# Two attention stages on one core: the end of the first attention reordered, and at the end of the second a bank for the last maxima and two sums through TensorE and ScalarE

## What is computed

```python
tgt2 = heads16_attention(x, ctx, Wq, Wk, Wv)[0]
y = x + tgt2
norm_X = layernorm(ctx, norm1)
norm_F_L = layernorm(y, norm2)
attended = attention(norm_F_L, norm_X, norm_X, 256 ** -0.5)      # first attention
h = gelu(attended @ fc1_w.T + fc1_b)                              # width 4
cross_attended = h @ fc2_w.T + fc2_b
norm_cross = layernorm(cross_attended, norm3)
self_attended = attention(norm_cross, norm_cross, norm_cross, 256 ** -0.5)   # second attention
out = norm_F_L + gamma2 * (cross_attended + gamma1 * self_attended)
```

## Time and profile before

| | us |
|---|---|
| median of 3 runs | 238.35 |
| lowest and highest | 234.89, 239.81 |
| profiled execution, its own time | 236.88 |
| its span, first to last instruction | 234.8 |
| PE, DVE, ACT, POOL busy in it | 209.6, 182.5, 153.8, 146.7 |

### The profile page before, as it was taken

The page is one execution under the profiler, slowest core; times in us unless marked ns, Lnnn a source line. Parts: engine busy times, 40 slices in busy tenths (PEclk is TensorE's granted clock), DMA queues, the critical chain, the costliest instruction groups (busy, mean ns, idle before and its releaser), DMA issues.

```text
span 234.8 us, 4965 instructions
## 1 busy us (share of the span) xinstructions
PE 209.6 (89%) x1730; PEld 151.6 (65%) x1730; DVE 182.5 (78%) x360; ACT 153.8 (66%) x295; POOL 146.7 (62%) x240
## 2 busy tenths in 40 slices
PE   8999979987779999999999989997998898899760
PEld 8776646776556978789787867794766444454230
DVE  6499977779979988878778999993333867988673
ACT  2177865544546877778777896789558786677520
POOL 6536551467499999987987793934953288322320
PEclk9999999999999999999999999999999999999855
DMA  6990000084540554426535200000000004444458
GB/s 227 384 332 4 1 1 3 0 223 138 178 179 3 179 179 138 149 78 180 179 108 158 94 3 0 6 0 1 3 0 0 3 15 167 179 181 180 183 212 324
DMA packets 14712, 26.81 MB, mean 114 GB/s; under 512 B 1760, under 2 KB 1760, under 8 KB 14688
## 3 DMA queue, kind: packets, MB, share of 16 engines
q1 hardware_dynamic: 14400, 25.98, 32.3%
q10 hardware_dynamic: 288, 0.52, 0.7%
HBM read 18.11 MB, written 8.39 MB: 113 GB/s over the span
## 4 chain that ended last, share of the span: by engine, by line
PE 53%; DVE 20%; ACT 10%; POOL 8%; issue 6%; DVEq 0%; ACTq 0%; POOLq 0%
PE psum L1085 15%; PE psum L1022 9%; PE psum L1093 5%; DVE xN L381 4%; DVE bn L361 4%; PE psum L970 3%; PE psum L1123 3%; DVE Fall L596 2%; DVE hmax L399 2%; PE psum L1105 2%; PE psum L1205 2%; DVE nmax L523 2%; ACT L862 2%; PE psum L1238 1%; ACT E L887 1%
## 5 line engine op out<-in xcount | busy, mean ns | idle before, releaser
L1085 PE MATMUL psum<-XT,Fall 128*128 128x256 f32 x256 | 61.0, 381 | 1.7 <-ACT Fall L857 1.7
L1085 PEld LDWEIGHTS psum<-XT,Fall 128*128 128x128 f32 x256 | 46.1, 190 | 7.3 <-ACT Fall L857 2.3
L700 POOL TENSOR_SCALAR cN<-cN,nmean,rstd 128x256 f32<-128x256 f32 x64 | 37.4, 594 | 2.5 <-POOL rstd L687 2.1
L680 POOL TENSOR_TENSOR xN<-xN,tgt 128x512 f32<-128x512 f32 x28 | 35.6, 1277 | 4.8 <-DVE xN L381 4.8
L687 POOL TENSOR_TENSOR rstd<-vps,minus_half 128x8 f32<-128x8 f32 (+1 forms) x16 | 24.2, 1512 | 19.9 <-DVE vps L372 19.6
L887 ACT ACTIVATE E<-psum,nmax 128x256 f32<-128x256 f32 x64 | 26.8, 474 | 11.9 <-DVE nmax L523 11.9
L880 ACT ACTIVATE PT<-psum 128x512 f32<-128x512 f32 x32 | 19.1, 598 | 22.7 <-PE psum L1093 22.6
L523 DVE TENSOR_REDUCE nmax<-psum 128x2 f32<-128x512 f32 x32 | 22.0, 687 | 14.7 <-PE psum L1085 14.2
L381 DVE TENSOR_SCALAR xN<-xN,bn,rstd 128x256 f32<-128x256 f32 x64 | 32.8, 558 | 0.5 <-POOL rstd L687 0.4
L581 DVE TENSOR_REDUCE nm<-psum 128x4 bf16<-128x1024 f32 x16 | 19.5, 1220 | 8.2 <-PE psum L1173 8.2
L854 ACT ACTIVATE XT<-psum,b1s,w1s 128x512 f32<-128x512 f32 x32 | 23.0, 795 | 4.0 <-PE psum L1022 4.0
(11 more groups left out here) (173 smaller groups left out, 351.9 us busy)
## 6 DMA issues: line engine op xcount, KB each, us to landing
cN<-ctx SPq DMA_DIRECT2D x32, 256.0 KB, 3.0
xN<-x SPq DMA_DIRECT2D x32, 256.0 KB, 4.1
out<-Fall SPq DMA_DIRECT2D x32, 256.0 KB, 2.3
x0T<-x0t ACTq DMA_DIRECT2D x1, 256.0 KB, 3.0
c0T<-c0t ACTq DMA_DIRECT2D x1, 256.0 KB, 3.9
wqT<-wqt SPq DMA_DIRECT2D x1, 256.0 KB, 3.6
wkT<-wkt SPq DMA_DIRECT2D x1, 256.0 KB, 4.1
wvT<-wvt SPq DMA_DIRECT2D x1, 256.0 KB, 4.8
```

Source lines behind the costliest of these rows:

```text
L680: pool.tensor_tensor(xN[:, b % SLOTS, :], xN[:, b % SLOTS, :], tgt2[:, :, :].rearrange("p t d -> p (t d)"), ALU.add).then_inc(y_ok, 1)
L700: pool.tensor_scalar(own, own, nmean[:, p % 4, NT * m + t:NT * m + t + 1], root_of(p, 0, m, t), ALU.add, ALU.mult)\
L1085: last = pe.matmul(bank[SBANK1[b % 3]][:, t * N:(t + 1) * N], Fall[:, b, c, t * P:(t + 1) * P], XT[:, p % 4, c, m * N:(m + 1) * N], start= ...
```

## The change

The program of PE, ACT and DVE is reordered at the end of the first attention and at the start of the second, and the end of the second attention gets three things: `maxima_turn(15)` writes in bank 3, once `weights(14)` has read that bank, and no longer in bank 5; the sums of pairs 13 and 15 leave DVE, in that PE first loads `Fall` into their result banks by matmuls with the identity (`load`), `output` adds onto that, and ACT copies the sum back over `Fall` (`moved`); and SP waits for `moved_ok` for these two pairs, in the same order of stores as before.

```diff
+    LOADED = (13, 15)
+    def maxima_bank(p):
+        return bank[3 if p == PAIRS - 1 else 5][0:2 * VW, 0:P // 2].bitcast(BF16)
...
         for n, b in ((n, b) for n in STORED for b in (2 * n, 2 * n + 1)):
-            sp.wait_ge(fin_ok, n + 1 + (b == B - 1))
+            if n in LOADED:
+                sp.wait_ge(moved_ok, 2 * LOADED.index(n) + b % 2 + 1)
+            else:
+                sp.wait_ge(fin_ok, min(n, 13) + 1)
...
         def finish(n):
             dve.wait_ge(f_mm, n + 1)
-            if n < PAIRS - 1:
-                dve.tensor_tensor(pair(n), results(n), pair(n), ALU.add).then_inc(fin_ok, 1)
-            else:
-                for m in range(2):
-                    own = Fall[:, 2 * n + m, :, :].rearrange("p c n -> p (c n)")
-                    dve.tensor_tensor(own, bank[result(n)[m]], own, ALU.add).then_inc(fin_ok, 1)
+            dve.tensor_tensor(pair(n), results(n), pair(n), ALU.add).then_inc(fin_ok, 1)
         maxima(0)
-        saved(QUADS - 1)
...
-            if p >= 5:
+            if p >= 5 and p - 5 not in LOADED:
                 finish(p - 5)
             if p == 0:
+                saved(QUADS - 1)
                 hidden_input(2)
...
-            if b >= 1:
+            if 1 <= b < B - 2:
                 weights_copied(b - 1)
+            if b == B - 3:
+                turned_values(QUADS - 1)
             exponentials(b)
-            if b % 4 == 1 and q >= 1:
+            if b % 4 == 1 and 1 <= q < QUADS - 1:
                 turned_values(q)
             if b % 4 == 2 and q >= 1:
                 applied(q - 1)
+            if b >= B - 2:
+                weights_copied(b - 1)
...
+        def moved(n):
+            act.wait_ge(f_mm, n + 1)
+            for m in range(2):
+                act.activation(Fall[:, 2 * n + m, :, :].rearrange("p c n -> p (c n)"), bank[result(n)[m]], ACT.Copy)\
+                    .then_inc(moved_ok, 1)
         for p in range(2 * QUADS + 4):
-            if p < PAIRS:
+            if p < PAIRS - 1:
                 maxima_turned(p)
             if p == 0:
+                weights(0)
                 applied(QUADS - 1)
+            if p + 2 < PAIRS:
+                turned(p + 2)
+            if 1 <= p < PAIRS:
+                weights(p)
             if p == 1:
                 hidden(2)
-            if p + 2 < PAIRS:
-                turned(p + 2)
-            if p < PAIRS:
-                weights(p)
+            if p == PAIRS - 2:
+                maxima_turned(PAIRS - 1)
             if p % 2 == 0 and 2 <= p < 2 * QUADS + 2:
                 collected((p - 2) // 2)
-            if p % 2 == 0 and p >= 4:
+            if p == PAIRS - 1:
+                output_turned((p - 5) // 2)
+            elif p % 2 == 0 and p >= 4 and p != PAIRS - 2:
                 output_turned((p - 4) // 2)
+        for n in LOADED:
+            moved(n)
...
         def maxima_turn(p):
             pe.wait_ge(max2_ok, p + 1)
-            if p >= 3 and p % 2 == 1:
+            if p == PAIRS - 1:
+                pe.wait_ge(exp2_ok, PAIRS - 1)
+            elif p >= 3 and p % 2 == 1:
                 pe.wait_ge(o2T_ok, (p - 1) // 2)
...
+        def load(n):
+            if n == 13:
+                pe.wait_ge(m_ok, PAIRS)
+            else:
+                pe.wait_ge(exp2_ok, PAIRS)
+            for m in range(2):
+                for c in range(DC):
+                    pe.matmul(bank[result(n)[m]][:, c * N:(c + 1) * N], ident[:, :], Fall[:, 2 * n + m, c, :],
+                              start=c == 0, stop=False, skip_group_check=True)
...
-            if b < B:
+            if b < B - 1:
                 score(b)
...
-            if b == 31:
-                scores(0)
+            if b == B - 2:
+                score(B - 1)
...
-            if b == 31:
+            if b == B - 1:
+                scores(0)
                 turn(1)
...
             if p == 0:
-                keep_busy(3, 6)
-                apply(QUADS - 1)
-            if p + 1 < PAIRS:
-                scores(p + 1)
-            if p == 0:
+                shift(0)
+                apply(QUADS - 1)
+                turn(2)
+                keep_busy(3, 5)
                 apply_back(QUADS - 1)
...
-                    keep_busy((5, 13)[p], 5)
-            if p == 2 * QUADS:
+                    if p == 1:
+                        keep_busy(13, 5)
+            if p == 2 * QUADS - 1:
+                back(QUADS - 2)
+                load(13)
+                output(p - 5)
+            elif p == 2 * QUADS:
                 attend(QUADS - 1)
                 output(p - 5)
                 back(QUADS - 1)
                 output_turn(QUADS - 2)
+                load(15)
```

More of the change, by code:

```diff
@@ L195, in build @@
     operand_ok = sem("operand_ok")
+    moved_ok = sem("moved_ok")
     h_ok, co_ok, sC_ok, pads_ok = sem("h_ok"), sem("co_ok"), sem("sC_ok"), sem("pads_ok")
@@ L926, in maxima_turned @@
                 act.wait_ge(s2m_mm, p - 1)
-            act.activation(nm2T[:, p % 2, :], bank[5][0:2 * VW, 0:P // 2].bitcast(BF16), ACT.Copy).then_inc(m_ok, 1)
+            act.activation(nm2T[:, p % 2, :], maxima_bank(p), ACT.Copy).then_inc(m_ok, 1)
         def weights(p):
@@ L1183, in maxima_turn @@
                 pe.wait_ge(co_ok, (p - 2) // 2)
-            pe.transpose(bank[5][0:2 * VW, 0:P // 2].bitcast(BF16), nm2[:, p % 2, :, :].rearrange("p m r -> p (m r)"),
+            pe.transpose(maxima_bank(p), nm2[:, p % 2, :, :].rearrange("p m r -> p (m r)"),
                          identb[:, :]).then_inc(m_mm, 1)
@@ L1211, in back @@
             pe.wait_ge(o2T_ok, q + 1)
-            pe.wait_ge(m_ok, min(2 * q + 4, PAIRS))
+            pe.wait_ge(m_ok, min(2 * q + 4, PAIRS - 1))
             for t in range(NT):
@@ L1230, in output @@
                 pe.wait_ge(fin_ok, 13)
-            elif n in (13, 15):
-                pe.wait_ge(exp2_ok, PAIRS)
-            elif n >= 1:
+            elif 1 <= n < 13:
                 pe.wait_ge(fin_ok, n)
@@ L1238, in output @@
                     last = pe.matmul(bank[result(n)[m]][:, c * N:(c + 1) * N], RT[rows, c * P:(c + 1) * P],
-                                     cT[rows, (n // 2) % 2, (n % 2) * N:(n % 2 + 1) * N], start=True, stop=True)
+                                     cT[rows, (n // 2) % 2, (n % 2) * N:(n % 2 + 1) * N], start=n not in LOADED,
+                                     stop=True, skip_group_check=n in LOADED)
             last.then_inc(f_mm, 1)
+        def load(n):
[7 more added lines that the diff above has]
+                              start=c == 0, stop=False, skip_group_check=True)
         for b in range(B + 1):
@@ L1283, in _ @@
             if p == 0:
+                shift(0)
+                apply(QUADS - 1)
+                turn(2)
+                keep_busy(3, 5)
                 apply_back(QUADS - 1)
-            if p + 2 < PAIRS:
-                turn(p + 2)
-            if p < PAIRS:
-                shift(p)
-                if p < 2:
-                    keep_busy((5, 13)[p], 5)
-            if p == 2 * QUADS:
+            else:
+                if p + 2 < PAIRS:
+                    turn(p + 2)
+                if p < PAIRS:
+                    shift(p)
+                    if p == 1:
[5 more added lines that the diff above has]
+            elif p == 2 * QUADS:
                 attend(QUADS - 1)
```

## The result

The changed kernel is slower: 239.76 us median of 20 executions (236.53 to 242.84), against 237.22 (234.89 to 241.43, 20 executions) for the kernel before; ratio 1.0076, 95% interval 1.0038 to 1.0113. The forecast was 237.1, 0.35 us faster, with a range up to 240.0: the time lies in the range, the sign is wrong. The ratio leaves out the executions furthest above the fastest, while the medians here are of all of them, since the spread is part of the story.

A forecast was written before the change was run, and what follows sets the result against it. The prediction took the final store block behind finish(12), and ahead of it POOL's chain, to bound the kernel; start -1.0 and end +0.65 gave -0.35 from a mean of 237.5, so 237.1 us, range 234.4 to 240.0.

The forecast's parts named there:

- The views: Profile views of the last 75 us: DMA showed the last eight stores as one solid block at 385 GB/s.
- end rule: Kernel end: execution ends at finish(12) plus 7.3 us (0.9 + 5.45 + 0.9), set by the stores of pairs 12 to 15.
- The start: Passage between the attentions: reordering starts POOL's chain 1.0 us earlier, bounds nothing to 1.1.
- The layout: Passage between the attentions: new programs timed with old durations, putting the turned weights 31 copy at 170.15, 1.1 us early.
- So 1.0 us is carried to the end: Second attention: POOL's 15.06 us chain is untouched and later order kept to `weights(14)`, so the start's 1.0 us gain persists.
- rival 1: Second attention's start: PE idles 2.1 us, clock may fall; the 1.0 and up to 1.0 more lost, say 238.6; chance 0.2.
- The end: End of the second attention: partly exposed loads of 1.9 us each make finish(12) 0.65 us later.
- Rival 2: Kernel end: loads run at granted clock 0.50, 3.8 us each, giving 241.8 us; chance 0.07.
- Rival 3: Kernel end: loads are hidden, taking 1.0 us or covered by the cT wait, giving 236.5 us; chance 0.2.
- Rival 4: Whole kernel: filling PE at 162.8 to 164 and the end steadies the clock, median 234.5 us; chance 0.08.
- The rule on the transfer rate: Final stores: by the skill's 341 GB/s the block lasts 6.15 us and the kernel ends 0.35 later, not earlier.
- Within 2%: Whole kernel: time differs from the kernel before by under 2%, 4.8 us; chance 0.91.

The follow-up runs named there:

- E3: The changed kernel with eight constant matmuls behind `attend(0)`, filling PE's 2.09 us gap: 234.88 us, ratio 0.9939.
- E4: The kernel before with the first part of the change alone, plus eight constant matmuls behind `attend(0)`: 234.33 us, ratio 0.9928.
- E6: E3 with the load and moved sum of pair 15 only, pair 13's sum back on DVE: 235.6 us, ratio 0.9983.
- E9: E7 with three constant matmuls added behind `back(6)` near the end: 233.35 us, ratio 0.9893.
- E2: The changed kernel with the first part (passage between the attentions) undone, so only the end is changed: 237.72 us, ratio 1.0043.
- E1: The kernel before with the first part alone (passage between the attentions), old end kept: 238.37 us, ratio 1.0038.
- E7: E4 with the result banks of the last pairs given out anew, so output(12) need not wait for finish(11): 233.82 us, ratio 0.9897.
- E10: E7 with three constant matmuls in place of eight behind `attend(0)`: 239.9 us, six executions from 232.84 to 241.58.
- E8: Control: the kernel before with two constant matmuls behind `attend(0)`: 237.11 us, ratio 1.0035.
- E5: E3 without the loads, sums 13 and 15 back on DVE, the rest of the new end order kept: 235.25 us, ratio 0.9977.

## Why the prediction was wrong

**The views and the end rule: right.** The end is that of finish(12) plus 7.3 us in all: 234.8 - 227.5 before, 235.0 - 227.74 after, 232.9 - 225.67 in E3, 231.6 - 224.29 in E4, 235.3 - 228.0 in E6. It holds as long as the block starts with pair 12; in E9 it starts with pair 11. The two sums taken off DVE bought nothing, as the prediction said.

**The start: right in kind, too small.** The term was 1.0 us with 1.1 as its upper bound; measured at the first `co` it was 1.58, outside the bounds. `weights(1)` started 14.28 us behind score(30) (174.78 - 160.50), not 14.86, and these 0.58 us are the whole excess. The bound had failed ahead of that: the copy that the layout put at 170.15, 1.1 us early, starts at 169.32, which is 1.6 early with the offset. The layout set the groups end to end, while the time order has each start some 0.1 us before the end of the one ahead; that this makes the whole difference is likely and not shown. The GELU ended 0.6 us earlier than laid out, and it was not on the path: POOL waited 4.12 us for it, and after that 4.30 for `co`.

**"So 1.0 us is carried to the end": this is the step that failed.** Nothing arrived. The changed kernel was 1.92 us ahead at the first `output_cuts`; finish(8) starts at 215.56, 0.11 ahead of the old kernel's 215.67, which with the offset of 0.34 is a loss of 0.23 since score(30). The sentence took for granted that POOL's chain sets the pace behind the first `co`. In its place stood rival 1, given 0.2: the gap of 2.1 us that the layout found was there with 2.09, the clock fell behind it, and PE at 0.51 became the limit in POOL's place: POOL waited 1.21 us for the second `co`, the lead at the third `output_cuts` was 0.41 (199.47 - 198.72 less the offset), and at the fourth it was gone. The rival had the mechanism and the place, and its cost in the profiled execution (1.81 us lost between the first `co` and finish(8), for some 2 laid out). What it lacked was the other executions: thirteen of twenty were 2 to 6 us worse than the profiled one, and the median is 239.76 where the rival said 238.6. In E3, with the gap filled, first `output_cuts` to finish(8) takes 29.67 us, against 29.52 before and 31.33 in the changed kernel: all but 0.15 comes back. The prediction itself had said that the rows do not tell what a longer gap does; that was a reason to weigh this rival as heavily as the forecast, and 0.2 was too little.

**The end: +0.65 forecast, +0.37 measured** from finish(9) to finish(12) (9.93 against 9.56 us), with the loads at 1.89 and 1.95 for an estimate of 1.9. But this compares with an old kernel that lost 0.83 to its own low clock. Between two kernels at full clock it is 1.19. That is the term whose base was mis-set: the walk took the old times with the low clock in them and gave the new kernel the full one. Over the executions of E2, the end alone, the ratio is 1.0043, 1.0 us. So of the two terms, -1.0 and +0.65, the first came out at +0.9 (E1, with an interval that holds 0) and the second at +1.0.

**Rival 2** (loads at the low clock, 3.8 us each) did not show in the profiled execution of the changed kernel, and E6 shows that it exists, with 3.73 us. Rival 3 needed loads of 1.0 us, and they took 1.9. Rival 4, a steadier clock, went the other way for the change and is what E3, E4, E7 and E9 had.

**The rule on the transfer rate.** The Trainium skill, "DMA: Bandwidth & Descriptors", section Bandwidth, gives 341 GB/s for a transfer of 1 MB and less for smaller ones. Its table is of transfers from HBM to SBUF that GpSimd issues, so it does not measure what happens here. In the changed kernel too the eight stores of 256 KB, which SP issues, ran at 385 and took 5.5 us as one block, and the trace decides.

**The chances.** Within 2% had 0.91 and came true.

## What to carry to other kernels

A reorder that brings work forward also moves the waiting. Where it leaves TensorE idle for longer than any wait of the old profile in that stage, price the clock first, and fill the gap with constants into a bank that nobody uses: here eight of them were worth 4.9 us of the median. Compare the end of two kernels only at the same clock: the old end took 9.56 us at a low clock and 8.74 at the full one. One profiled execution shows one draw of the clock; a change in idle time shows in the spread of twenty. And where stores run back to back at the end, count bytes backwards from the end: the instruction ahead of the block is on the path, those inside it are free as long as each is done before its store can begin.

## What the runs showed of the hardware that was not expected

- The same program, with one gap of 1.22 us, took 232.84 or 241.58 us (E10). With the gap closed, ten executions lay within 1.1 us (E7), while the kernel before ranged from 234.9 to 241.7 in the same series.
- In four kernels the fall of the clock stood in four places of one stage: at 184 (changed kernel, at 0.51 until 190.7), 182 to 189 (E1), 202 to 209 (E2), 196 to 203 (E8), with 1.00 on both sides of it. In the first two it came behind the wait of 2.09 us; in E2 and E8 no wait of PE between 190 us and the fall was longer than 0.68.
- The clock at the end differs from kernel to kernel too, and these profiles do not tie it to the loads: it was 1.00 up to 228 us in the changed kernel and up to 226 in E1 and E8, and 0.50 or little more from about 220 on in E5, E6 and E7.
- f32 matmuls of 128x256 take 1.89 to 1.95 us for four at 1.00 and 3.73 at 0.50 (E6), and `attend` 1.05 and 1.89: at half clock these groups take close to twice their time, while the short bf16 groups go from 0.39 to 0.61.
- Open: where in the executions of 240 us and more the low clock lies. The traces are of faster ones, and for the others there is only the mean clock of each.
